# Four chained attention layers: last attention by query halves, reciprocal broadcast on two row groups, sums of x from its update, a new order of steps

## The chip, the cores and the metric

The kernel runs on one core of one Trainium2 chip. TensorE does matrix products out of SBUF into PSUM, ScalarE (ACT) and VectorE (DVE) work on both memories, GpSimd (POOL) on SBUF alone, and the SyncE queue (SP) issues the DMAs. The engines run independently and meet only at semaphores. The metric is the device time of one execution in microseconds (us), lower is better.

## What is computed

x has 2 images of 128 channels by 32x32 positions. Four layers of attention follow each other, each adding its result to x. Positions are 1024 queries and 1024 keys (256 keys in layer 2, which pools 2x2 first).

```python
# layer 0: 4 heads of 4 channels, softmax over the query axis
S = einsum('bhdn,bhdm->bhnm', q, k);  A = softmax(S, axis=-2)
o = einsum('bhdn,bhnm->bhdm', v, A);  x = gamma * (Wo o + bo) + x
# layer 1: one head, 16 channels for q and k, 128 for v
attn = softmax(q k, axis=2);          x = x + gamma * (v attn)
# layer 2: 8 heads of 16; q from group_norm(x), k and v from group_norm(avg_pool2(x))
x = x + wproj @ (softmax(q k * scale) v)
# layer 3: one head of 128 channels on group_norm(x, 32 groups)
x = x + out_w @ (softmax(q k * scale) v) + out_b
```

## The kernel before

**Units.** The work is cut into 17 attention units (L, b, g): layer, image, and a group within the layer (heads in layers 0 and 2; layer 3 of image 0 has its keys split into two units). The last unit is (3, 1, 0). Image 0 runs ahead of image 1, so that at most times two units are in the air.

**Steps of a unit.** The plan is a list of steps, in the kinds of the letters of the string `ORDER` (L89): N are projections q and k, statistics and norm; V is the projection v and one weight fold; A are 8 score tiles whose row maxima VectorE takes out of PSUM (L625 to L636, 1024 elements a row); T turns the maxima into a row (`top`), which a DMA writes next to the operands; B are 8 score tiles, now with the maximum subtracted by the product itself, of which ScalarE takes the exponential into the ring `P` of 13 buffers (L518); P are the products of probabilities and v into `acc` (`PV4` L904 for layers 0 and 2; `PV1` L910 for layers 1 and 3, one per key tile t and half h of the 512 queries), and `out`, the copy of `acc` to SBUF (L529); E is the epilogue. In the epilogue, `den` sums the probabilities on TensorE (L930), VectorE takes the reciprocal and splits it in two parts (L650 to L654), `bcast` spreads it over the channels by 8 products of 128 columns (L939), VectorE multiplies by it and adds to x. In layers 1 and 3 the probabilities are first added up tile by tile into `DS` (L380): on GpSimd for key tiles 1 to 5, on VectorE for 6 and 7.

**What sets the order.** Every engine walks the same list `plan` in its order and takes its own part of each step; nothing is reordered at run time, except that GpSimd only does its sums and SP only its DMAs. Every step that needs PSUM takes the next of three PSUM slots of 1024 columns (`RING`), in plan order; TensorE waits until the step three places before has been read. A new string `ORDER` therefore moves work on TensorE, ScalarE and VectorE at once.

**Places the change touches.** Layer 0's q is masked into two copies (`q0_parity`, L485) on ScalarE after VectorE wrote both halves of it (L598); the first A of a unit waits for the copy (L812). `stats` of layers 2 and 3: ScalarE takes the mean of x (L541, layer 2 only) and its squares (L544) with an accumulating read-out; VectorE pools x (L704 to L710) or, in layer 3, sums x (L699). `norm` (L717 to L744) is a chain of some 15 small VectorE instructions, each waiting for the one before, followed by the scaled copy of x (L550) on ScalarE. x is updated in layer 1 and 3 by L680 (both tensors in SBUF) and in layer 2 by L685 (one tensor in PSUM). The end: the last `out` copies 1024 columns, L674 multiplies, L680 adds, L416 writes 512 KB to memory.

## Time and profile before

| | |
|---|---|
| median of 3 runs | 391.42 us (388.67 to 391.69) |
| the profiled execution | 388.21 us |
| its span, first to last instruction | 386.2 us |
| busy: TensorE, VectorE, ScalarE, GpSimd | 348.5, 255.8, 191.8, 52.4 us |
| mean granted TensorE clock | 0.962 of full speed |

The span is 2.0 us shorter than the execution's own time. Busy time of TensorE is modelled: a matmul's record reaches from its start to its last result, and successive ones overlap, so a row "x8 in 3.43 us" of the chain of waits is the better price of a group than its mean duration. Each fp32 matmul leaves two records. "Idle before" is the idle time of the engine ahead of a row, and the arrow names what ended it.

### The profile page before, as it was taken

To read this page: it belongs to the slowest core of one execution; us is meant where nothing else is said; L and a number is where in the kernel's file an instruction comes from. 1 tells how busy PE (TensorE), PEld (TensorE's weight loads), DVE (VectorE), ACT (ScalarE), POOL (GpSimd) and SP (SyncE) were. 2 spreads that over 40 slices of the span, in tenths; PEclk is the share of its full clock that TensorE was granted. 3 is DMA by queue.
4 is the path that set the end of the run, shared out by engine and by line. 5 is a ranking of instruction groups with operands and counts; after the bars stand their busy time and mean duration, and the time that the engine had idled before them with its cause. 6 is when DMAs were issued, how large, how long until landed. Compare 5 with 4: busy or idle time off the path is not lost.

```text
span 386.2 us, 4574 instructions
## 1 busy us (share of the span) xinstructions
PE 348.5 (90%) x1766; PEld 157.3 (41%) x1766; DVE 255.8 (66%) x315; ACT 191.8 (50%) x234; POOL 52.4 (14%) x36
## 2 busy tenths in 40 slices
PE   8869898999899986999999789969999996999993
PEld 5523322344234432454434335534442453555541
DVE  2799877869878664888773559884981165790424
ACT  4705777685762497545665152256056714224221
POOL 5000000000026300000002142022200022005420
PEclk9955999999999999999999999998999998999998
DMA  8000000000000000000000000000000000000101
GB/s 300 9 0 2 0 3 1 2 0 0 2 0 2 0 0 3 1 3 0 3 0 2 0 0 0 2 0 1 3 2 3 0 0 0 2 0 2 54 0 54
DMA packets 1316, 4.43 MB, mean 11 GB/s; under 512 B 176, under 2 KB 528, under 8 KB 1168
## 3 DMA queue, kind: packets, MB, share of 16 engines
q1 hardware_dynamic: 1296, 4.15, 2.9%
q8 instruction: 14, 0.23, 0.2%
q14 instruction: 6, 0.05, 0.0%
HBM read 2.99 MB, written 1.05 MB: 10 GB/s over the span
## 4 chain that ended last, share of the span: by engine, by line
PE 71%; DVE 18%; ACT 6%; issue 4%; DVEq 0%; ACTq 0%
PE attn_acc L910 13%; PE attn_acc L904 11%; PE products L875 8%; DVE neg_max L632 5%; PE products L879 5%; PE products L825 4%; PE products L864 4%; PE products L793 3%; PE products L869 3%; PE products L797 3%; PE products L838 2%; PE products L939 2%; PE products L805 2%; ACT probs L518 2%; DVE neg_max L635 2%
## 5 line engine op out<-in xcount | busy, mean ns | idle before, releaser
L518 ACT ACTIVATE probs<-products 128x1024 f32<-128x1024 f32 x128 | 126.8, 1022 | 79.2 <-PE products L885 33.7
L632 DVE TENSOR_REDUCE neg_max<-products 128x2 f32<-128x1024 f32 x64 | 75.7, 1219 | 17.6 <-PE products L825 17.6
L910 PE MATMUL attn_acc<-probs,v 128*128 128x512 f32 x128 | 62.7, 607 | 0.0
L904 PE MATMUL attn_acc<-probs,v 128*32 128x512 f32 x384 | 51.1, 612 | 0.4 <-ACT probs L518 0.4
L380 POOL TENSOR_TENSOR prob_sum<-prob_sum,probs 128x1024 f32<-128x1024 f32 x16 | 37.6, 2351 | 77.6 <-ACT probs L518 76.9
L380 POOL TENSOR_TENSOR prob_sum<-probs 128x1024 f32<-128x1024 f32 x4 | 9.4, 2354 | 238.8 <-ACT probs L518 238.8
L635 DVE TENSOR_REDUCE neg_max<-products 128x1 f32<-128x1024 f32 x32 | 37.9, 1220 | 5.7 <-PE products L830 3.7
L629 DVE TENSOR_REDUCE neg_max<-products 128x4 f32<-128x1024 f32 x32 | 37.5, 1217 | 4.5 <-PE products L838 4.4
L910 PEld LDWEIGHTS attn_acc<-probs,v 128*128 128x128 f32 x128 | 22.4, 189 | 21.3 <-issue 18.8
L879 PE MATMUL products<-rows_a,rows_b 128*128 128x512 f32 x64 | 30.5, 599 | 0.6 <-ACT probs L518 0.5
L650 DVE RECIPROCAL recips<-products 128x128 f32<-128x128 f32 x10 | 9.5, 955 | 24.1 <-PE products L930 24.1
L529 ACT ACTIVATE attn_out<-attn_acc 128x512 f32<-128x512 f32 (+1 forms) x16 | 13.0, 814 | 23.3 <-PE attn_acc L910 16.3
L825 PE MATMUL products<-q_even,rounded_a 64*128 64x512 f32 x64 | 17.7, 569 | 3.8 <-DVE neg_max L632 2.6
L864 PE MATMUL products<-rounded_a,q_even 64*128 64x512 f32 x64 | 16.3, 520 | 2.5 <-DVE neg_max L632 1.4
L793 PE MATMUL products<-x_norm,w 128*128 128x512 f32 x16 | 10.3, 729 | 8.9 <-ACT x_norm L550 8.9
L825 PE MATMUL products<-rounded_b,rounded_a 64*128 64x512 f32 x64 | 17.1, 535 | 0.7 <-ACT probs L518 0.5
L380 DVE TENSOR_TENSOR prob_sum<-prob_sum,probs 128x1024 f32<-128x1024 f32 x8 | 9.8, 1221 | 11.2 <-POOL prob_sum L380 6.9
L879 PEld LDWEIGHTS products<-rows_a,rows_b 128*128 128x128 f32 x64 | 11.8, 189 | 12.4 <-issue 10.7
L875 PE MATMUL products<-rows_a,k_rows 64*128 64x512 f32 x64 | 16.3, 612 | 0.5 <-DVE neg_max L629 0.4
L885 PE MATMUL products<-max_rows,max_picker 128*128 128x512 f32 x32 | 16.1, 586 | 0.1
L869 PE MATMUL products<-rows_a,rows_b 64*128 64x512 f32 x64 | 15.9, 606 | 0.0
L864 PE MATMUL products<-rounded_a,rounded_b 64*128 64x512 f32 x64 | 14.1, 458 | 1.9 <-DVE neg_max L632 1.4
(133 smaller groups left out, 410.6 us busy)
## 6 DMA issues: line engine op xcount, KB each, us to landing
w<-w_rest SPq DMA_DIRECT2D x1, 1235.5 KB, 7.5
x<-x SPq DMA_DIRECT2D x2, 512.0 KB, 4.2
y<-x SPq DMA_DIRECT2D x2, 512.0 KB, 2.6
tmp<-row_selector SPq DMA_DIRECT2D x1, 512.0 KB, 8.3
w<-w_first SPq DMA_DIRECT2D x1, 147.0 KB, 2.2
rounded_a<-max_rows SPq DMA_DIRECT2D x8, 4.0 KB
rows_a<-max_rows SPq DMA_DIRECT2D x4, 2.0 KB
rows_a<-max_rows SPq DMA_DIRECT2D x2, 16.0 KB
```

The costliest lines, as they stand in the source:

```text
L380: engine.tensor_tensor(DS[:, :], first_in, P[:, n % NP, :], ALU.add).then_inc(den_acc, 1)
L518: nc.scalar.activation(P[:, n % NP, :], slot(s), ACT.Exp, scale=SCALE[L]).then_inc(read_act, 1)
L629: nc.vector.tensor_reduce(out=m2, in_=slot(s).rearrange("p (a i k) -> p a i k", a=2, i=2), op=ALU.max, axis=AX.X, negate=True).then_inc(re ...
L632: nc.vector.tensor_reduce(out=m[:, 2 * t:2 * t + 2], in_=slot(s).rearrange("p (a n) -> p a n", a=2), op=ALU.max, axis=AX.X, negate=True).t ...
L635: nc.vector.tensor_reduce(out=m[:, t:t + 1], in_=slot(s), op=ALU.max, axis=AX.X, negate=True).then_inc(read_dve, 1)
L825: mm = nc.tensor.matmul(slot(s)[:, halves[a]], RA[b][rows, tile], q0_parity(b, g // 2)[rows, halves[nh]], start=True, stop=True)
L864: mm = nc.tensor.matmul(slot(s)[:, halves[a]], q0_parity(b, g // 2)[rows, 128 * t:128 * (t + 1)], RA[b][rows, halves[g % 2]], start=True, ...
L869: mm = nc.tensor.matmul(slot(s)[:, h], FB[b][rows, 128 * t:128 * (t + 1)], FA[b][rows, h], start=True, stop=True)
L875: mm = nc.tensor.matmul(slot(s)[:, halves[a]], KF2[b][rows, hp, g, 128 * kt:128 * (kt + 1)], (FA, FB)[g][b][rows, halves[half]], start=Tru ...
L879: nc.tensor.matmul(slot(s)[:, h], FB[b][:, 128 * t:128 * (t + 1)], FA[b][:, h], start=True, stop=False)
L904: mm = nc.tensor.matmul(acc[32 * j:32 * j + 32, h], lhs, P[:, b_no[q] % NP, halves[a]], start=t0 == 0 if L == 0 else t0 % 2 == 0, stop=t0 ...
L910: mm = nc.tensor.matmul(acc[:, h], V13[b][:, t0, :], P[:, b_no[q] % NP, h], start=t0 == first, stop=t0 == last)
```

## The change

It has five parts.

1. **Last attention by query halves.** In the last unit all 8 products for queries 0 to 511 are issued first, then those for 512 to 1023. A new step `oh` copies the first half of `acc` in between. Multiply, add and output DMA are done for each half.
2. **Reciprocal broadcast on two 64-row groups.** The 8 products of each `bcast` take 64 rows each and are issued alternately to rows 0 to 63 and 64 to 127.
3. **Sums of x from its update.** The updates of x in layers 1 and 2 also put out the sum of x. ScalarE's pass L541 goes, VectorE's pass L699 becomes a copy of one column; layer 2 gets one small scaling instead.
4. **q masks by halves.** Layer 0's masked copies of q are made by halves, and the first of them waits for the first half of q only.
5. **A new order of steps.**

```diff
 ORDER = (
-    "NNVNNAVAAAAAAAATAAABABABABAABAPTBABPABABAPBABABABA"
...
-    "AAPAPPAAVAPAPTAAAPPABBABBAPABPTBBBPBBBPPBBBBBPEPPP"
-    "EEPBEYENBNPBNNPPAAPPAABAAPAAVPTPPEBBBPBBEPPPPPPBBP"
-    "PPPBPPPPEPEP"
+    "NNVAANANAVAAAAATAAABAABABABAABPTBAABAPBABABAPBABBA"
...
+    "PAAAPAAPVPAAPTAAPAAPBBABBAPABPTBBBPBBPBBBPBBBPEPPP"
+    "EPEYEBENPPNBBNNVAAPAPAAPAABAPPTPPEBBBBBPPBPPPBBPPP"
+    "EEPPPPPPPPEPP"
 )
...
+        if (L, b) == LAST:
+            steps["P"] += [("PV1", L, b, g, t, 0) for t in range(8)] + [("oh", L, b, g)] + [
+                ("PV1", L, b, g, t, 1) for t in range(8)]
...
+                elif kind == "bcast" and (L, b) == LAST:
+                    for i, h in enumerate(halves):
+                        sp.wait_ge(x_upd, x_no[(3, b)] + i)
+                        sp.dma_start(out[b][:, h], X[b][:, h]).then_inc(out_done, 16)
...
-                        wait_read(act, s)
                         for p in range(2):
-                            nc.scalar.activation(q0_parity(b, p)[:, :], RB[b][:, :].bitcast(F32), ACT.Identity,
-                                                 scale=w("group_mask")[:, p:p + 1]).then_inc(q0_masked, 1)
+                            for h in halves:
+                                if p == 0 and h.start == 0:
+                                    act.wait_ge(q0_lo_half, q0_no[s] + 1)
+                                elif p == 0:
+                                    wait_read(act, s)
+                                nc.scalar.activation(q0_parity(b, p)[:, h], RB[b][:, h].bitcast(F32), ACT.Identity,
+                                                     scale=w("group_mask")[:, p:p + 1]).then_inc(q0_masked, 1)
...
+                elif kind == "oh":
+                    u = s[1:]
+                    act.wait_ge(pv_done, half_pv)
...
+                    nc.scalar.activation(O[o_tile[u]][:, halves[0]], acc[:, halves[0]], ACT.Identity).then_inc(half_out, 1)
+                elif kind == "out" and (L, b) == LAST:
+                    u = s[1:]
+                    act.wait_ge(pv_done, pv_done_at[("B", *u, 7)])
+                    nc.scalar.activation(O[o_tile[u]][:, halves[1]], acc[:, halves[1]], ACT.Identity).then_inc(acc_out, 1)
...
-                    if L == 2:
-                        nc.scalar.activation(unused, X[b][:, :], ACT.Identity, scale=1.0 / N,
-                                             accum_out=mv[:, 0, 0:1]).then_inc(act_chain, 1)
-                        act.wait_ge(act_chain, b + 1)
...
+                    elif (L, b) == LAST:
+                        wait_read(dve, ("fold", 3))
+                        if x_upd_before(s):
+                            dve.wait_ge(x_upd, x_upd_before(s))
+                        for i, h in enumerate(halves):
+                            if i == 0:
+                                dve.wait_ge(half_out, 1)
+                            else:
+                                dve.wait_ge(acc_out, out_no[("out", L, b, g)] + 1)
+                            link(nc.vector.tensor_tensor(T[:, h], o[:, h], slot(s)[:, h], ALU.mult))
+                            nc.vector.scalar_tensor_tensor(out=X[b][:, h], in0=T[:, h], scalar=b3eff[:, 0:1],
+                                                           in1=X[b][:, h], op0=ALU.add, op1=ALU.add).then_inc(x_upd, 1)
...
+                            nc.vector.scalar_tensor_tensor(out=X[b][:, :], in0=T[:, :], scalar=gb1[:, 0:1],
+                                                           in1=X[b][:, :], op0=ALU.add, op1=ALU.add,
+                                                           accum_out=xsum[:, b:b + 1]).then_inc(x_upd, 1)
...
-                    nc.vector.tensor_tensor(X[b][:, :], slot(s), X[b][:, :], ALU.add).then_inc(read_dve, 1)
+                    nc.vector.scalar_tensor_tensor(out=X[b][:, :], in0=slot(s), scalar=1.0, in1=X[b][:, :],
+                                                   op0=ALU.mult, op1=ALU.add,
+                                                   accum_out=xsum[:, b:b + 1]).then_inc(read_dve, 1)
...
-                        nc.vector.tensor_reduce(out=mv[:, 0, 0:1], in_=X[b][:, :], op=ALU.add,
-                                                axis=AX.X).then_inc(stats_done, 1)
+                        nc.vector.tensor_copy(mv[:, 0, 0:1], xsum[:, b:b + 1]).then_inc(stats_done, 1)
...
+                    nc.vector.tensor_scalar(mv[:, 0, 0:1], xsum[:, b:b + 1], 1.0 / N, None, ALU.mult)
...
-                            pe.wait_ge(q0_masked, 2 * q0_no[("q", 0, b)] + g // 2 + 1)
+                            pe.wait_ge(q0_masked, 4 * q0_no[("q", 0, b)] + 2 * (g // 2) + 1)
...
+                    if L == 0 and t == 1:
+                        pe.wait_ge(q0_masked, 4 * q0_no[("q", 0, b)] + 2 * (g // 2) + 2)
...
-                    for t in range(NT):
-                        mm = nc.tensor.matmul(slot(s)[:, 128 * t:128 * (t + 1)], selr[:, t, :], RT[:, :],
-                                              start=True, stop=True)
+                    for i in range(NT // 2):
+                        for a in range(2):
+                            t = NT // 2 * a + i
+                            rows = slice(WIDE * a, WIDE * a + WIDE)
+                            mm = nc.tensor.matmul(slot(s)[:, 128 * t:128 * (t + 1)], selr[rows, t, :], RT[rows, :],
+                                                  start=True, stop=True)
```

Written out as steps, these are the stretches of the new order in which the prediction's steps lie (b0 and b1 are the images; steps not named keep their places but for a few swaps of neighbours):

```
start    before  k00 q00 v00 k01 q01 A0 v01 A1 A2 A3 A4
         after   k00 q00 v00 A0 A1 k01 A2 q01 A3 v01 A4
L2 b0    before  q200 k20 B34 out012 v20 PV40130 B35 A0 A1 PV40131
         after   q200 k20 B34 out012 PV40130 PV40131 B35 A0 v20 A1
end L2   before  out201 B0 B1 B2 den201 PV00 ya20 bcast201 PV01 PV10 y20 stats30 B3 PV11 PV20 norm30
 b0      after   out201 B0 den201 B1 B2 B3 bcast201 ya20 PV00 y20 PV01 PV10 PV11 stats30 PV20 norm30
norm21   before  stats21 B3000 B3001 norm21 B3002 PV00 q210
         after   stats21 B3000 B3001 norm21 PV00 PV01 B3002 q210
norm31   before  out211 B3014 bcast211 ya21 y21 stats31 B3015 norm31 PV40 B3016 q31 k31 PV41
         after   out211 den211 ya21 bcast211 B3014 y21 stats31 PV40 PV41 norm31 B3015 B3016 q31 k31 v31
end      before  B0 B1 B2 PV00 B3 B4 bcast301 PV01 .. B7 PV51 PV60 PV61 PV70 den310 PV71 bcast310 out310
         after   B0 .. B4 PV00 PV10 B5 PV20 PV30 PV40 B6 B7 PV50 PV60 PV70 bcast301 den310 oh PV01 .. PV61 bcast310 PV71 out310
```

## Rows read from the trace of the kernel before

**Rows 1.** The page: busy time of each engine, and two lines of slices.
```profile
PE 348.5 (90%) x1766; PEld 157.3 (41%) x1766; DVE 255.8 (66%) x315; ACT 191.8 (50%) x234; POOL 52.4 (14%) x36
PEclk9955999999999999999999999998999998999998
```
**Rows 2.** Windows: us, PE, PEld, DVE, ACT, POOL busy, clock, DMA share, GB/s.
```profile
16.00:48.00 32.00, 25.57 (x110) 10.29 (x111) 28.99 (x30) 14.78 (x16) 0.00 (x0) 0.68 0.00 1
48.00:80.00 32.00, 29.23 (x199) 9.96 (x199) 25.94 (x27) 24.49 (x31) 0.00 (x0) 1.00 0.01 2
```
**Rows 3.** Timeline of the start: start us, us, engine, line, tiles, idle before.
```profile
10.64 1.15 ACT L485 ACTIVATE q_even<-rounded_b,w 128x1024 fp32r<-128x1024 f32 x1 [0.89 <-DVE rounded_b L598]
13.60 1.42 DVE L598 SCALAR_TENSOR_TENSOR rounded_a<-products,w,stage_hi 128x512 fp32r<-128x512 f32 x2 [2.64 <-ACT stage_hi L474]
16.27 1.22 DVE L632 TENSOR_REDUCE neg_max<-products 128x2 f32<-128x1024 f32 x1
```
**Rows 4.** Chain that ended last, pieces in time: start us, us, what.
```profile
123.08 1.06 PE attn_acc L910 x2
203.49 1.04 PE products L939 x8
312.15 0.84 PE products L939 x8
352.50 0.86 PE attn_acc L910 x2
```
**Rows 5.** Timeline: products on two 64-row groups, layer 2.
```profile
280.64 1.04 PE L838 MATMUL products<-k_rounded,rounded_b 64*128 64x256 f32 x12
```
**Rows 6.** Timeline, norm and v of image 0 in layer 2.
```profile
142.78 1.06 ACT L541 ACTIVATE x_norm<-x 128x1024 bf16<-128x1024 f32 x1 [0.21 <-DVE x L680]
144.65 0.22 DVE L710 SCALAR_TENSOR_TENSOR mean_var<-mean_var 128x1 f32<-128x1 f32 x1
145.25 0.36 PE L965 MATMUL products<-mean_var,w 128*128 128x4 f32 x2 [1.51 <-ACT x_norm L544]
154.27 0.71 PE L805 MATMUL products<-w,kv_norm 128*128 128x128 f32 x4 [1.04 <-DVE rows_a L602]
```
**Rows 7.** Timeline, end of layer 2 of image 0, den201 and bcast201.
```profile
209.50 2.35 POOL L380 TENSOR_TENSOR prob_sum<-probs 128x1024 f32<-128x1024 f32 x1 [80.57 <-ACT probs L518]
211.97 2.51 DVE L654 SCALAR_TENSOR_TENSOR recip_rows<-recips_hi,w,recips 128x128 fp32r<-128x128 f32 x1
214.58 1.08 PE L939 MATMUL products<-recip_rows,head_rows_to_channels 128*128 128x128 f32 x8 [2.08 <-issue]
```
**Rows 8.** Timeline, norm30.
```profile
222.58 2.35 POOL L380 TENSOR_TENSOR prob_sum<-prob_sum,probs 128x1024 f32<-128x1024 f32 x1 [8.25 <-ACT probs L518]
222.72 2.22 DVE L732 SCALAR_TENSOR_TENSOR norm_tmp<-norm_tmp,eps 128x1 f32<-128x1 f32 x1
227.98 1.10 PE L793 MATMUL products<-x_norm,w 128*128 128x512 f32 x2 [1.92 <-ACT x_norm L550]
```
**Rows 9.** Timeline, norm31.
```profile
319.93 2.33 DVE L732 SCALAR_TENSOR_TENSOR norm_tmp<-norm_tmp,eps 128x1 f32<-128x1 f32 x1
325.30 1.46 PE L793 MATMUL products<-x_norm,w 128*128 128x512 f32 x2 [2.70 <-ACT x_norm L550]
326.55 1.91 PE L797 MATMUL products<-x_norm,w 128*128 128x512 f32 x2
```
**Rows 10.** Timeline, the end.
```profile
377.67 1.12 PE L910 MATMUL attn_acc<-probs,v 128*128 128x512 f32 x2
378.83 1.02 ACT L529 ACTIVATE attn_out<-attn_acc 128x1024 f32<-128x1024 f32 x1 [4.04 <-PE attn_acc L910]
381.89 1.28 DVE L680 SCALAR_TENSOR_TENSOR x<-tmp,b3eff,x 128x1024 f32<-128x1024 f32 x1
```
**Rows 11.** Groups by line and form: busy us, mean ns.
```profile
L604 DVE TENSOR_SCALAR rows_b<-products,w 128x512 f32<-128x512 f32 x8 | 5.9, 749 | 2.3 <-PE products L793 1.5 <-ACT rounded_b L479 0.6
L529 ACT ACTIVATE attn_out<-attn_acc 128x512 f32<-128x512 f32 x8 | 4.8, 604 | 2.1 <-PE attn_acc L904 2.1
```

More of the change, by code:

```diff
@@ L74 @@
 TILES[(3, 0, 0)], TILES[(3, 0, 1)] = range(0, 4), range(4, 8)
+LAST = (3, 1)
 def groups(L, b):
@@ L138, in build_plan @@
         steps["B"] += [("B", L, b, g, t) for t in TILES[(L, b, g)]]
-        steps["P"] += [("PV4", L, b, g, c) for c in range(4)] if L in (0, 2) else [
-            ("PV1", L, b, g, t, h) for t in TILES[(L, b, g)] for h in range(2)]
+        if (L, b) == LAST:
+            steps["P"] += [("PV1", L, b, g, t, 0) for t in range(8)] + [("oh", L, b, g)] + [
+                ("PV1", L, b, g, t, 1) for t in range(8)]
+        else:
+            steps["P"] += [("PV4", L, b, g, c) for c in range(4)] if L in (0, 2) else [
+                ("PV1", L, b, g, t, h) for t in TILES[(L, b, g)] for h in range(2)]
         steps["P"] += [("out", L, b, g)]
@@ L194, in attention_layers @@
             o_tile[s[1:]] = o_tile[(*s[1:3], s[3] - 1)]
-        elif s[0] == "out":
+        elif s[0] == "oh" or s[0] == "out" and s[1:3] != LAST:
             tile, before = free.pop(0)
@@ L204, in attention_layers @@
     for s in plan:
+        if s[0] == "PV1" and s[1:3] == LAST and s[4:] == (7, 0):
+            n += 1
+            half_pv = n
         if s[0] == "PV4" or s[0] == "PV1" and s[5] == 1:
@@ L270, in attention_layers @@
         eps = sb("eps", [C, 2])
+        xsum = sb("x_sums", [C, B])
         zeros = sb("zeros", [128, NKV])
@@ L293, in attention_layers @@
         acc_out = sem("acc_out")
+        half_out = sem("half_out")
         recip_done = sem("recip_done")
@@ L600, in _ @@
                                 in1=HT[:, split0.index(s) % 2, h].bitcast(F32), op0=ALU.add, op1=ALU.add)
+                            if kind == "q" and h.start == 0:
+                                lo.then_inc(q0_lo_half, 1)
                         elif L == 2:
@@ L911, in _ @@
                                               start=t0 == first, stop=t0 == last)
-                    if kind == "PV4" or s[5] == 1:
+                    if kind == "PV4" or s[5] == 1 or (L, b) == LAST and t0 == 7:
                         mm.then_inc(pv_done, 1)
```

29 lines of the change are left out of this document (18 added, 11 removed).

## Prediction

> **What bounds the kernel now.** I read the page first. TensorE is busy 348.5 of 386.2 us, VectorE 255.8, GpSimd 52.4, and the second line shows the TensorE clock at its lower level, 1.2 GHz, in slices 2 and 3 of 40 (about 19 to 39 us) and dipping near 260 and 325 us [rows 1]. So TensorE sets the time, and what can be won is its idle time, its time at the lower clock, and the ends of the kernel. Next come the windows: from 16 to 48 us VectorE is the fuller engine (28.99 of 32 us against TensorE's 25.57), from 48 to 80 us TensorE is (29.23) [rows 2]. Then the chain of waits, for what a group of products costs back to back [rows 4, 5], and the timeline wherever TensorE idles [rows 3, 6 to 10].
>
> One pattern explains most of those places. A VectorE instruction on one column, normally 0.16 to 0.22 us, takes 2.22 us at 222.72, and it ends at 224.94, as the GpSimd sum that began at 222.58 does (2.35 us) [rows 8]. The same happens to L732 at 319.93 (2.33 us) [rows 9] and to L654, 2.51 us at 211.97, behind a row of GpSimd sums [rows 7]. All of these read SBUF alone. So a GpSimd sum that starts inside a chain of small VectorE instructions costs about 2.1 us, and TensorE pays: it idles 2.08 us before bcast201 [rows 7], 1.92 before norm30's q [rows 8] and 2.70 before norm31's [rows 9]. The step that starts such a sum is a B tile, so the order of steps decides whether they meet.
>
> **q masks by halves, and the start: -1.8 us.** VectorE finishes v00 at about 10.96 us, then idles 2.64 us until 13.60, because ScalarE makes two full masked copies (L485, 1.15 us the first) before it rounds k01; its first maximum starts at 16.27 [rows 3]. In the new order A0 and A1 stand ahead of k01, and the first half mask (about 0.6 us by the 512-wide copy [rows 11]) can start when VectorE has written half of q, some 0.8 us earlier. VectorE can then take two maxima (2 x 1.22 = 2.44 us) in the 2.64 us gap. All else it does up to the eighth maximum stays, and to 48 us it is the fuller engine [rows 2], so the whole is 2.4 us shorter at best. Two extra ScalarE launches are hidden by ScalarE's 14.78 of 32 us. Bounds 0 and -2.6. I take -1.8, since TensorE at 1.2 GHz is near full as well.
>
> **Broadcast on two row groups: -2.0 us.** A bcast is 8 products in 0.84 us between 128-row products and 1.04 us next to 64-row ones [rows 4], so 0.105 us each. Layer 2's products on two row groups, 12 of 256 columns, run in 1.04 us including the 0.27 us of the last one's latency, so 0.07 us each, with twice the columns [rows 5]. Eight of them then take 0.56 us at most; one streaming bound by half the columns gives 0.42. But the rows show a price of changing the row groups: a pair of L910 takes 0.86 us after its like and 1.06 us right after 64-row work [rows 4], 0.2 us a change. For the five or so bcasts next to 64-row work the change goes away, for those inside layer 3 it is added. Gain per bcast 0.1 to 0.5 us, taken as 0.28; of ten, nine count here (the last is in the end's sum), and about seven lie on TensorE's path: -2.0, bounds 0 and -4.
>
> The Trainium skill bears on this: "TensorEngine Tiling (Array Packing)", Key Properties, says that changing the tiling mode drains the engine. The 0.2 us rows agree with it. By that rule alone, bcasts among 128-row products win nothing.
>
> **Sums of x: +0.3 us.** In layer 2 ScalarE's L541 goes (1.06 us plus its read-out), but VectorE's pooling chain beside it ends at 144.65 + 0.22 = 144.87, and the norm product starts at 145.25 [rows 6]. With one small scaling more on VectorE that product starts only 0.1 us sooner. In layer 3 the pass that goes ran beside ScalarE's squares, so nothing is won there either. What is paid is the accumulating read-out on the four updates of x, 0.1 us each from nothing up to the 0.19 us ScalarE's needs by the groups. ScalarE is free 1.2 us earlier, but it only passes on exponentials for which TensorE isn't waiting.
>
> Another price for the update in layer 1, with both tensors in SBUF: the Trainium skill's "Vector Engine (DVE) Microarchitecture Reference", section 7, says such an instruction with two fp32 SBUF inputs and the accumulator runs at half throughput. No row shows one. It is rival 3.
>
> **L2 of image 0, v20 moved back: -0.6 us.** TensorE idles 1.04 us in front of v20, whose slot waits for VectorE [rows 6]. In the new order PV40130 and PV40131 stand there, 1.0 us each and ready. A0 still can't start before 156.4 us (k is then read), so TensorE wins one such product group less the v20 work (0.4 us) that it does later.
>
> **End of layer 2 of image 0: -3.6 us.** den201 now stands behind B0 instead of B2 and ahead of B1, whose exponential starts GpSimd's first sum. TensorE can start it once `out201` is copied, at 207.5 us. Reciprocal 0.96, rounding 0.23, split 0.35 then end near 209.9; B1's exponential would end near 210.2. So L654 runs free of GpSimd, by a margin of about 0.3 us, and B1 to B3 cover the wait: the 2.08 us of idle goes [rows 7]. After that B3 is done before `stats30`, and the next exponential stands behind norm30 in ScalarE's list, so no GpSimd sum falls into norm30's chain: 2.1 us less there, and the 1.92 us of idle goes [rows 8]. Together 4.0 us; 3.6 for crumbs. Bounds -0.3 (both holds come back) and -4.2.
>
> **norm21: -0.5 us.** One more PV stands between norm21 and q210, where TensorE idles 2.7 us, but the idle 0.46 ahead of norm21 is untouched and GpSimd's first sum still falls into the chain, earlier by about the time that ScalarE saves. Bounds 0 and -1.7 (the clock's dip at 260 us spared).
>
> **norm31: -2.8 us.** B3014 moves ahead of y21, and B3015, whose exponential started the sum that held L732, moves behind norm31 in every list. The chain ends 2.1 us sooner, and PV40, PV41 fill the wait for the statistics. Now q31 starts at 325.30 after 2.70 us of idle, and its second product pair takes 1.91 us where the same work takes 0.86 at 2.4 GHz: the granted clock there is at its lower level after the idle time [rows 9]. I put q31 at 323.8 (-1.5), one PV more done by then (-0.86), and about half of the 1.9 us that the lower clock costs the four products as spared. That is 3.3; 2.8 taken, bounds -1 and -4.5.
>
> **The end: -2.4 us.** Now from the end of the last PV (377.67 + 1.12 = 378.79) follow copy, bcast, multiply and add, until 381.89 + 1.28 = 383.17: 4.38 us [rows 10]. Then 3.0 us of DMA end the span. After: half copy 0.60 [rows 11], half multiply 0.7, half add 0.75 (as the 512-wide 0.749 of L604 [rows 11]), handoffs 0.15: 2.2 us, so -2.2. The last bcast now comes ahead of the last PV on TensorE (+0.5), and den310 no longer makes TensorE wait (0.76 us), as bcast301 is put ahead of it and covers the last sum: -0.7. The final DMA carries half; I leave its 3.0 us, since a latency may be all of it (else -0.6). The first half's DMA and image 0's, which is later now than at 362 us but still behind a full PV half of about 6 us, are hidden.
>
> **Sum.** -1.8 - 2.0 + 0.3 - 0.6 - 3.6 - 0.5 - 2.8 - 2.4 = -13.4, from the profiled 388.21: 374.8. The runs' median is 3.2 us above that execution, their lowest 0.5. A median of the new kernel may lie as high above its fastest, so I add 1.2: **376.0 us**. Its own range is 371 to 380.
>
> **Rivals.** Of the bounds above, no one alone changes the sign.
> 1. **Forecast**, chance 0.50.
> 2. **GpSimd's holds come back elsewhere**, 0.20. The margin at den201 is 0.3 us, and earlier exponentials make earlier sums. Two holds of 2.1 us with the idle time behind them give back 5: 381. For: the same holds at 211, 222 and 320 us. Against: the lists keep B behind the two norms.
> 3. **The accumulator halves the layer 1 update**, 0.10: L680 at 1.28 us [rows 10] becomes 2.56, twice on the path: 376.0 + 2.6 = 378.6. The Trainium skill's page named above would give this.
> 4. **Dependences take most of it**, 0.12. VectorE has 28.99 of 32 us in 16 to 48, so that start and norms move but their followers wait for VectorE. Start, v20, norm21 and half of norm31 and of the bcasts gone: 376 + 1.8 + 0.6 + 0.5 + 1.4 + 1.0 = 381.3; with rival 2 on top up to 386. This includes that splitting into row groups does nothing.
> 5. **The clock stays low**, 0.08, the case on the other side. It is at 1.2 GHz from 19 to 39 us while VectorE bounds. If the new mix of A and B keeps it there into 48 to 80, where TensorE is busy 29.23 of 32 us, each microsecond of its work costs nearly one more. From 14 us longer at the lower level it decides; 20 us give about 394.
>
> The range holds forecast and rivals 2 to 4: 369 to 386. About 1% is what can be told from no change here, so below 387.5 is faster: 0.85; within 1% 0.08 (rivals 4 and 5 mild); slower 0.07.
>
> **What would show it.** The first L632 near 11 to 12 us instead of 16.27. Bcasts of 0.5 to 0.6 us, and L910 pairs of 1.06 behind them in layer 3. L654 of bcast201 at 0.35 us and no idle before it; L732 at 0.16 us in norm30 and norm31, still one held op in norm21. No L541. L680 of layer 1 near 1.3 us, or 2.6 by rival 3. At the end 2.2 us from the last PV to the last add. I am wrong if the slices of the clock show the lower level past slice 3, or if TensorE's idle time before its q products stays.

## The result

| | before | after |
|---|---|---|
| median of 4 runs | 390.05 us (388.36 to 391.69) | 375.77 us (373.23 to 375.94) |
| the profiled execution | 388.21 us | 375.87 us |
| its span | 386.2 us | 373.8 us |
| mean granted TensorE clock in it | 0.962 | 0.965 |

The ratio is 0.961, with an interval of 0.956 to 0.967: 3.9% faster. The forecast of 376.0 us (range 369 to 386) holds. But it is a sum of eight terms, and what follows asks which of them were right. Two failed in this profile: the start, whose gain came out only in executions where the clock stayed up, and v20. The price of the sums of x was never separated, and the end was near in size with wrong parts.

To see where the time went I compare the starts of the same steps in the two profiled executions. The differences between columns are worked out from the timelines.

| step | before | after | ahead by |
|---|---|---|---|
| first maximum (VectorE) | 16.27 | 11.79 | 4.5 |
| fold behind the eighth maximum | 25.63 | 26.06 | -0.4 |
| norm product, layer 2 of image 0 | 145.25 | 145.20 | 0.0 |
| bcast200 | 203.42 | 203.65 | -0.2 |
| bcast201 | 214.58 | 210.56 | 4.0 |
| q30 | 227.98 | 223.24 | 4.7 |
| norm21 | 254.08 | 249.10 | 5.0 |
| q210 | 260.94 | 255.81 | 5.1 |
| norm31 | 319.09 | 312.78 | 6.3 |
| q31 | 325.30 | 317.44 | 7.9 |
| first B of the last unit | 345.68 | 335.63 | 10.0 |
| end of the last PV | 378.79 | 369.24 | 9.5 |
| end of the last add | 383.17 | 371.38 | 11.8 |
| end of the span | 386.2 | 373.8 | 12.4 |

So between these two executions nothing at all is won in the first 203 us, and everything in the last 170. This is the page of the kernel after, its engines and its clock, to set beside [rows 1]:

```profile
PE 344.5 (92%) x1766; PEld 153.3 (41%) x1766; DVE 244.8 (65%) x323; ACT 191.3 (51%) x235; POOL 52.4 (14%) x36
PEclk9875899999999999999999999998999999999998
```

TensorE is still the engine that bounds. Of the two dips of the clock behind norms, near 260 and 325 us before, one is left, the single 8 in the 28th slice, 252 to 262 us.

**The start** (timeline of after, columns as in [rows 3]):

```profile
11.79 2.36 DVE L663 TENSOR_REDUCE neg_max<-products 128x2 f32<-128x1024 f32 x2 [0.18 <-PE products L876]
13.91 1.91 PE L846 MATMUL products<-x,w 128*128 128x512 f32 x2
15.03 0.75 DVE L627 SCALAR_TENSOR_TENSOR rounded_a<-products,w,stage_hi 128x512 fp32r<-128x512 f32 x1 [0.88 <-ACT stage_hi L490]
16.73 0.75 DVE L627 SCALAR_TENSOR_TENSOR rounded_a<-products,w,stage_hi 128x512 fp32r<-128x512 f32 x1 [0.95 <-ACT stage_hi L490]
```

Two maxima do stand in the gap of [rows 3], as forecast. Then VectorE waits twice, 0.88 and 0.95 us, for k01's halves. The granted clock fell here: k01's second pair of records (L846) takes 1.91 us, where it takes 1.02 in the kernel before.

**The end of layer 2 of image 0, and the norm behind it** (timeline of after), to set beside [rows 7, 8]:

```profile
209.66 0.35 DVE L685 SCALAR_TENSOR_TENSOR recip_rows<-recips_hi,w,recips 128x128 fp32r<-128x128 f32 x1
210.56 2.37 POOL L392 TENSOR_TENSOR prob_sum<-probs 128x1024 f32<-128x1024 f32 x1 [82.02 <-ACT probs L538]
210.56 0.96 PE L993 MATMUL products<-recip_rows,head_rows_to_channels 64*128 64x128 f32 x8
...
220.04 0.16 DVE L781 SCALAR_TENSOR_TENSOR norm_tmp<-norm_tmp,eps 128x1 f32<-128x1 f32 x1
...
223.24 1.10 PE L842 MATMUL products<-x_norm,w 128*128 128x512 f32 x2
```

The split (L685 now) takes 0.35 us for 2.51 and is through 0.55 us before GpSimd's first sum starts; the one-column instruction takes 0.16 us for 2.22; TensorE idles neither before the broadcast nor before norm30's q.

**norm31 and norm21** (timeline of after), to set beside [rows 9]:

```profile
250.40 2.34 POOL L392 TENSOR_TENSOR prob_sum<-probs 128x1024 f32<-128x1024 f32 x1 [20.77 <-ACT probs L538]
250.47 2.41 DVE L776 SCALAR_TENSOR_TENSOR norm_tmp<-norm_tmp 128x1 f32<-128x1 f32 x2
255.81 2.05 PE L842 MATMUL products<-x_norm,w 128*128 128x512 f32 x2 [2.43 <-ACT x_norm L579]
...
313.62 0.16 DVE L781 SCALAR_TENSOR_TENSOR norm_tmp<-norm_tmp,eps 128x1 f32<-128x1 f32 x1
317.44 1.02 PE L842 MATMUL products<-x_norm,w 128*128 128x512 f32 x2
```

In norm21 one instruction is still held, as forecast, and TensorE idles 2.43 us behind it; its next pair of records takes 2.05 us. norm31 is free of it, and its pair takes 1.02 us.

**Sums of x** (timeline of after):

```profile
141.41 1.28 DVE L724 SCALAR_TENSOR_TENSOR x<-tmp,gamma_bv,x 128x1024 f32<-128x1024 f32 x1
142.62 0.08 DVE L724 DVE_READ_ACCUMULATOR x<-tmp,gamma_bv,x 128x1 f32 x1
```

The update with both tensors in SBUF takes 1.28 us as it did without the accumulator, and the read-out 0.08 us.

**The end** (chain that ended last, pieces in time: start us, us, what), to set beside [rows 10]:

```profile
360.23 0.59 PE products L993 x8
360.82 0.57 PE products L981 x16
361.39 6.21 PE attn_acc L961 x14
367.60 0.59 PE products L993 x8
368.19 1.07 PE attn_acc L961 x2
...
369.28 0.61 ACT attn_out L551
...
369.91 0.70 DVE tmp L710
...
370.63 0.75 DVE x L711
```

The pieces left out are of 0.02 us. From the last PV to the last add it is 2.1 us instead of 4.4. The DMA behind is 2.4 us (371.38 to 373.8) instead of 3.0, and its landing is on the page:

```profile
y<-x SPq DMA_DIRECT2D x1, 512.0 KB, 2.6
y<-x SPq DMA_DIRECT2D x2, 256.0 KB, 2.0
```

**One thing is needed to read the numbers below.** Executions of one and the same kernel differ by whole dips of the TensorE clock, that is stretches in which the granted clock falls toward its lower level, and such differences come to 2.5 us and more. Of the kernel before, six of the 13 executions measured along with experiment 1 have a mean granted clock of 0.961 or 0.962 and take 387.6 to 388.6 us; seven have 0.950 to 0.957 and take 391.4 to 393.1. Of the kernel after, one has 0.971 and takes 373.2 us, three have 0.965 and take 375.7 to 375.9. So medians carry luck of some 3 us, and I compare, beside the medians, executions of like mean clock or the fastest of each kernel, and steps of one profile against each other. The mean doesn't say where a dip lies, though: the profiles of experiments 1 and 6 have one at 152 to 164 us, where neither before nor after has one, and in experiment 4 the executions at a mean of 0.953 are faster than those at 0.958. A difference read at like clock is therefore good to about 1 us, and step distances are the better evidence. The lowest times of the two kernels in this comparison are 388.4 and 373.2 us, 15.1 apart (14.3 against 387.6, the lowest of before anywhere); the two profiled executions are 12.3 apart.

### The profile page after: what moved, and what is told of

Its sections match the earlier page's. It is cut to its first block, busy times and chain, and to the rows that moved or that the text cites. A ratio compares the mean times of both kernels' runs of the same rounds, so it can differ in the third digit from the quotient of the medians.

```text
span 373.8 us, 4592 instructions
## 1 busy us (share of the span) xinstructions
PE 344.5 (92%) x1766; PEld 153.3 (41%) x1766; DVE 244.8 (65%) x323; ACT 191.3 (51%) x235; POOL 52.4 (14%) x36
## 4 chain that ended last, share of the span: by engine, by line
PE 75%; DVE 14%; ACT 6%; issue 4%; ACTq 0%; DVEq 0%
PE attn_acc L961 13%; PE attn_acc L955 11%; PE products L926 7%; PE products L930 7%; PE products L915 5%; PE products L876 5%; PE products L842 4%; PE products L846 4%; PE products L920 4%; DVE neg_max L660 3%; DVE neg_max L663 3%; DVE neg_max L666 3%; ACT probs L538 3%; PE products L854 2%; PE products L1010 2%
## 5 line engine op out<-in xcount | busy, mean ns | idle before, releaser
L538 ACT ACTIVATE probs<-products 128x1024 f32<-128x1024 f32 x128 | 126.7, 1024 | 79.4 <-PE products L936 32.2
L562 ACT ACTIVATE attn_out<-attn_acc 128x512 f32<-128x512 f32 (+1 forms) x15 | 12.0, 800 | 17.1 <-PE attn_acc L961 11.6
L915 PE MATMUL products<-rounded_a,rounded_b 64*128 64x512 f32 x64 | 14.3, 464 | 1.6 <-ACT probs L538 1.0
L926 PE MATMUL products<-rows_b,k_rows 64*128 64x512 f32 x64 | 15.4, 605 | 0.0
```

What stands on the lines that cost most here:

```text
L538: nc.scalar.activation(P[:, n % NP, :], slot(s), ACT.Exp, scale=SCALE[L]).then_inc(read_act, 1)
L915: mm = nc.tensor.matmul(slot(s)[:, halves[a]], q0_parity(b, g // 2)[rows, 128 * t:128 * (t + 1)], RA[b][rows, halves[g % 2]], start=True, ...
L926: mm = nc.tensor.matmul(slot(s)[:, halves[a]], KF2[b][rows, hp, g, 128 * kt:128 * (kt + 1)], (FA, FB)[g][b][rows, halves[half]], start=Tru ...
```

## The experiments

### 1. The order against the rest

Two kernels split the change. The first is the kernel before with the new string up to the last unit:

```diff
 ORDER = (
-    "NNVNNAVAAAAAAAATAAABABABABAABAPTBABPABABAPBABABABA"
...
+    "NNVAANANAVAAAAATAAABAABABABAABPTBAABAPBABABAPBABBA"
...
```

> The kernel before, with the new order of steps up to the last unit and nothing else of the change. By the prediction the order carries the start (in part), the end of layer 2 of image 0, v20, norm21 and norm31: 388.2 - 7 to - 9, about 380. The traces of the two kernels say that nothing is won up to bcast200 at 203 us and 9 us from there to the first B of the last unit: bcast201 near 210.6, norm30's q near 223.5 to 224, the last unit's first B near 337 to 338 instead of 345.7, time 379 to 381. The rival, that the row groups and the sums of x carry the gain, expects over 385.

Measured: 381.78 us (381.44 to 383.18), 0.980 of before (0.974 to 0.986). The second has the row groups, the sums and the half masks, but the old order and end (here in its one line that differs beside the string):

```diff
-LAST = (3, 1)
+LAST = (9, 9)
```

> The new row groups of the broadcast, the sums of x from the update and the q masks by halves, with the old order and the old end. By the prediction -2.0 for the row groups and +0.3 for the sums: 386.5. By the traces of the two kernels the broadcasts are 0.2 to 0.3 us shorter each, the updates longer by 0.1, and little of it lies on the path: 386 to 388. If the parts carried the gain: under 383.

Measured: 385.39 us, in two pairs: 383.8 and 383.9 at a clock of 0.962, 386.9 twice at 0.957; 0.989 of before (0.982 to 0.995). At the clock of 0.962 the kernel before takes 388.2 (its middle), so these parts win 4.3 us, not the 1.7 that I had put down and not the 0 to 2 of the expectation. The row groups have 2.1 of it (experiment 6). The other 2 us are not assigned by any run: masks and sums were not run alone. The profile shows two candidates. The masks by halves bring the fold behind the eighth maximum 0.24 us nearer to v00 (16.61 us behind v00's first product, 16.85 before). And from norm31's product to the end of the span it is 64.4 us instead of 67.1: the held instruction costs 0.4 us less (norm31's product to q31 in 5.77 us for 6.21), and the clock stays at 1.00 behind it, where it dipped in the profile of before. Whether the new sums spare that dip or this execution merely drew none is open.

The order alone wins 6.6 at equal clock (381.5 against 388.1), less than the 7 to 9 of the expectation and than the 9.3 of the terms that it carries. The steps say where that goes: from bcast200 to the first B of the last unit its profile has 131.95 us, as after (131.98) and 10.3 less than before (142.26), but it reaches bcast200 only at 207.55, with a low clock at 12 to 16 and at 152 to 160 us. With the end's 1.8 (experiment 7) the three differences make 12.7, near the 12.3 of the two profiled executions; as each is good to about 1 us, that they add up so well is in part luck.

### 2. The end of layer 2 of image 0, alone and undone

The new order of these steps put into the kernel before:

```diff
-    "BBABAAPANAVNTPBABABABABAPAPBBAPABEPTBBEPPPBBBEPYEP"
-    "PENBPPNBBPPNNBBAAPAPAPAPAPPPPAPEAPVETNBBNBPNNNBAAP"
+    "BBABAAPANAVNTPBABABABABAPAPBBAPABEPTBBEPPPBEBBBEYP"
+    "EPPPNPNBBPPNNBBAAPAPAPAPAPPPPAPEAPVETNBBNBPNNNBAAP"
```

These are the steps of the stretch "end L2 b0".

> The kernel before, with 12 steps in the new order: from behind B0 to norm30 at the end of layer 2 of image 0 (den201 ahead of B1, B3 ahead of the broadcast). Theory (GpSimd's sums held L654 and L732): L654 at 0.35 us, L732 at 0.16 us, TensorE's 2.08 and 1.92 us of idle time gone, norm30's q near 224 instead of 228, and the same 3.5 to 4.5 us at the end: about 384.3. Rival (the gain is given back behind, since VectorE or GpSimd bounds the next stretch): norm30's q at 224, but under 2 us at the end.

Measured: 386.45 us (382.24 to 387.04), 0.989 of before (0.981 to 0.997). In its profile no L654 above 0.35 us and no held L732 in norm30. From bcast200 to norm21 it takes 253.59 - 207.26 = 46.33 us, where before takes 254.08 - 203.42 = 50.66: 4.3 us. From bcast200 to the last add it is 173.75 for 179.75; the 1.7 more are a dip behind norm21 that this execution doesn't have and before has. At 0.957, the clock of two of its executions, it takes 386.9, before 391.4: 4.5.

The same steps undone in the changed kernel:

```diff
-    "BAPABBAAPANBTPAAVBABABBAPAPBBAPABEPTBBEPPPBEBBBEYP"
-    "EPPPNPNBBPPNPNBB...
+    "BAPABBAAPANBTPAAVBABABBAPAPBBAPABEPTBBEPPPBBBEPYEP"
+    "PENBPPNBBPPNPNBB...
```

> The changed kernel with the 12 steps at the end of layer 2 of image 0 in the old order (den201 behind B2, B3 behind stats30). By the prediction 3.6 us more, by the two traces 4 to 4.7: 377 beside 373.2 where the clock's dip near 256 us stays away, 379.5 to 380 beside 375.8 where it comes; L685 held to 2.5 us and L781 to 2.2 us again. Rival (the gain is one of idle time that another stretch would have had): under 2 us.

Measured: 381.98 us (378.29 to 382.37). Best against best 378.29 - 373.23 = 5.1 us, by the medians 6.2; the steps are worth more than the 3.6 forecast. The holds are back (timeline of this kernel):

```profile
209.01 2.35 POOL L392 TENSOR_TENSOR prob_sum<-probs 128x1024 f32<-128x1024 f32 x1 [81.04 <-ACT probs L538]
210.30 1.14 DVE L684 CAST recips_hi<-recips 128x128 fp32r<-128x128 f32 x1
211.47 2.51 DVE L685 SCALAR_TENSOR_TENSOR recip_rows<-recips_hi,w,recips 128x128 fp32r<-128x128 f32 x1
214.09 0.66 PE L993 MATMUL products<-recip_rows,head_rows_to_channels 64*128 64x128 f32 x8 [2.08 <-issue]
221.82 2.34 POOL L392 TENSOR_TENSOR prob_sum<-prob_sum,probs 128x1024 f32<-128x1024 f32 x1 [7.98 <-ACT probs L538]
221.96 2.23 DVE L781 SCALAR_TENSOR_TENSOR norm_tmp<-norm_tmp,eps 128x1 f32<-128x1 f32 x1
```

The same two idle times of TensorE, 2.08 us here and 1.92 before q30, return with them. Put in or taken out, the steps are worth 4.3 to 5.1 us, so the gain belongs to them and isn't given back behind them.

### 3. Are the holds GpSimd's doing?

```diff
-POOL_SUM = 6
+POOL_SUM = 1
```

All sums of probabilities go to VectorE, in the kernel before:

> The kernel before with all sums of probabilities on VectorE (POOL_SUM 1 for 6), GpSimd idle after its memsets. Theory (GpSimd's sums hold VectorE instructions that read SBUF alone): L653 and L654 at 0.23 and 0.35 us, L732 and L740 at 0.16, and q30, q210, q31 each about 2 us sooner. VectorE does 20 sums of 1.22 us more, 24 us, some of it in the way where it is full: between 381 and 390. Rival (something else holds them, a semaphore of the chain or the PSUM): they stay at 2.2 us.

Measured: 386.33 us (385.33 to 386.51), 0.989 of before (0.983 to 0.995), at a clock of 0.952 to 0.953. No instruction of the chains is held (timeline of this kernel):

```profile
214.26 0.35 DVE L654 SCALAR_TENSOR_TENSOR recip_rows<-recips_hi,w,recips 128x128 fp32r<-128x128 f32 x1
224.04 0.16 DVE L732 SCALAR_TENSOR_TENSOR norm_tmp<-norm_tmp,eps 128x1 f32<-128x1 f32 x1
227.24 1.10 PE L793 MATMUL products<-x_norm,w 128*128 128x512 f32 x2 [0.28 <-ACT x_norm L550]
```

The stretches behind the norms shrink by what the holds cost: from norm21's product to q210 4.72 us for 6.86, from norm31's to q31 4.04 for 6.21. With 24 us more of sums on VectorE (its busy time rises by 10.6 only, 266.4 for 255.8) this kernel is 1% faster than the one before. In the changed kernel the same edit (POOL_SUM = 1 for 6) has little left to win:

> The same in the changed kernel, where one instruction is still held (2.41 us in norm21). Theory: that one falls to 0.35, q210 comes 2 us sooner and the clock's dip behind it goes, for 2 to 4 us less, against 24 us more of VectorE work in layers 1 and 3, where the new order has put no room for it: 371 to 378. In the last unit the sums have time (VectorE idles 18.7 us ahead of the sixth).

Measured: 381.37 us (380.46 to 381.69), 5.6 us slower than the changed kernel and above what I expected. norm21's hold is gone, but norm21 itself comes later: from bcast201 it is 42.6 us away (253.16 - 210.57) instead of 38.5. The sums of layer 1's image 1 now stand among the maxima of layer 3's image 0 on VectorE, and TensorE idles 2.53 us before `den` (L981, at 241.28) for the last of them. So the holds are GpSimd's, shown in both kernels, and the cure depends on the order: before, take the sums away from GpSimd; after, move their start.

Not every instruction is held. In experiment 4's second kernel a GpSimd sum runs from 311.68 to 314.06; two one-column instructions of the form TENSOR_SCALAR inside it take 0.15 and 0.14 us (L783, L785, at 311.88 and 311.95), and the SCALAR_TENSOR_TENSOR behind them is held for 1.95. The prediction's words "all of these read SBUF alone" are true of the held ones, but it is not enough to be held.

The Trainium skill has the rule: "GPSIMD Engine Reference", sections 1 and 8, says that GpSimd shares its SBUF interfaces with VectorE and contends with instructions that have two SBUF inputs or run in a two-port mode. The trace agrees for two inputs (L732 at 2.22 us). The cast L653 has one input and takes 1.14 us beside a sum, 0.23 elsewhere; whether it runs in a two-port mode no row shows. A hold costs here what is left of a sum of 2.35 us.

### 4. norm31 alone and undone

The new order from norm31 on to the last unit, put into the kernel before:

```diff
-    "EEPBEYENBNPBNNPPAAPPAABAAPAAVPTPPEBBBPBBEPPPPPPBBP"
+    "EPEYEBENPPNBBNNVAAPAPAAPAABAPPTPPEBBBPBBEPPPPPPBBP"
```

> The kernel before, with the steps between the last broadcast of layer 2 of image 1 and the last A of the last unit in the new order. By the prediction -2.8, by the two traces -3.3 to -3.7 (no held L732, no lower clock over the q products, v31 in the wait for the first A): about 384.7. Rival (most of it came from the shorter broadcasts and the lower clock spared by chance): under 1.5 us.

Measured in ten executions: four take 384.7 to 385.2 us at a clock of 0.965, four 388.5 to 389.1 at 0.953, two 389.9 at 0.958; 0.992 of before (0.987 to 0.997). Its fast four against the fast six of before that is 3.2 us less (384.9 against 388.1). From norm31's product to the last PV's end its profile has 55.95 us, before 59.70: 3.75, and it has no dip behind norm31.

And the reverse in the changed kernel:

```diff
-    "EPEYEBENPPNBBNNVAAPAPAAPAABAPPTPPEBBBBBPPBPPPBBPPP"
+    "EEPBEYENBNPBNNPPAAPPAABAAPAAVPTPPEBBBBBPPBPPPBBPPP"
```

> The changed kernel with the steps from the last broadcast of layer 2 of image 1 to v31 in the old order. By the prediction 2.8 us more, by the two traces 3.3 to 3.7: 376.5 to 377 with no dip at 256 us, 379 with one; L781 held in norm31, and a dip of the clock behind it. Rival (the order only moved idle time): under 1.5 us.

Measured: 376.99 us (375.17 to 377.59), by the medians 1.2 us more than after, below the 1.5 that the rival would leave. But medians mix dips. Its best is 1.9 us above the best of after, and its profiled execution, with a dip of the clock behind norm31 as in [rows 9] and none behind norm21, is 4.0 above. In that profile the held instruction and what follows it are these:

```profile
312.13 1.95 DVE L776 SCALAR_TENSOR_TENSOR norm_tmp<-norm_tmp 128x1 f32<-128x1 f32 x1
316.60 2.05 PE L842 MATMUL products<-x_norm,w 128*128 128x512 f32 x2 [2.26 <-ACT x_norm L579]
318.44 1.80 PE L846 MATMUL products<-x_norm,w 128*128 128x512 f32 x2
```

So the steps are worth the hold, about 1.9 us, and about 2 more in executions where the clock would have dipped.

### 5. The start

The old first ten steps in the changed kernel:

```diff
-    "NNVAANANAVAAAAATAAAB...
+    "NNVNNAVAAAAAAAATAAAB...
```

> The changed kernel with the first ten steps in the old order; masks of q by halves stay. By the prediction the start was worth 1.8 us: 377.7. By the trace of the changed kernel, whose eighth maximum is no sooner than before (26.06 us against 25.63) since k01 and q01 run at 1.2 GHz there, it is worth nothing: 375.9, with the eighth maximum at 26.0 to 26.5.

Measured: 373.42 us (372.96 to 376.22), of which three at a clock of 0.971, where after has one (373.23). Equal at equal mean clock. I count the start from v00's first product, since the kernels' first products come at 5.06 to 5.62 us. The fold behind the eighth maximum is 16.62 us behind it with the old start, 16.63 in the profile of after, 16.85 in the kernel before. In that profile the start's new order is worth nothing.

Why? In the changed kernel the clock fell to 0.65 in 12 to 16 us, under k01's products. So I kept TensorE busy there with products whose results are unused:

```diff
-    "NNVAANANAVAAAAATAAAB...
+    "NNVAWAWNWAWNAVAAAAATAAAB...
```

> The changed kernel with four idle products (128x256, fp32, 0.43 us each at 2.4 GHz, results unused) after A0, A1, k01 and A2 of the first unit, nothing else. Theory: the start won nothing because TensorE's clock fell at about 12.6 us, when it had only v00's 16-column products and waits; kept busy it stays at 2.4 GHz until q01 is done, the eighth maximum comes at 24 to 25 us instead of 26.06 and the whole is 1 to 2 us shorter. Rival (the start is bound by ScalarE's rounding and masks): the eighth maximum stays at 26, or moves later by the added products.

Measured: 375.83 us (372.84 to 376.29), no change. The clock did stay at its upper level (windows of this kernel: us, TensorE busy, clock, DMA share, GB/s):

```profile
12.00:16.00 4.00, 4.00 (x14) 1.00 0.00 0
16.00:20.00 4.00, 4.00 (x21) 1.00 0.00 0
```

and the fold still came at 26.00 us. VectorE's waits in that kernel: 1.11 us in ScalarE's wait for k01's product, 1.07 in VectorE's for the rounding, then 1.57 and 0.47 us for q01. A0 and A1 wait for the masks on TensorE, and k01, which stood right behind v00 before (10.2 to 10.5 us), is queued behind them until 12.6.

This looks like the end of the theory of the clock, but the test changes two things: the idle products stand ahead of k01 and q01. k01 starts 3.87 us behind v00 here, and 3.16 in after; q01 7.08, and 7.04 in after with its slow clock. The theory has a cleaner test in two kernels run for other reasons, which have the same first unit as after: the one with the old end (experiment 7) and the one without GpSimd's sums (experiment 3). In both the clock stayed up by itself. The windows, after first, then the old end and no GpSimd sums:

```profile
12.00:16.00 4.00, 3.84 (x8) 0.65 0.00 0
12.00:16.00 4.00, 3.59 (x12) 1.00 0.00 0
12.00:16.00 4.00, 3.60 (x11) 1.00 0.00 0
```

And the rows of the one with the old end (timeline; v00's first product is at 9.73, k01's at 12.90, q01's at 15.24):

```profile
13.86 1.02 PE L846 MATMUL products<-x,w 128*128 128x512 f32 x2
14.94 1.61 DVE L627 SCALAR_TENSOR_TENSOR rounded_a<-products,w,stage_hi 128x512 fp32r<-128x512 f32 x2 [0.49 <-ACT stage_hi L490]
24.89 0.17 DVE L674 TENSOR_TENSOR max_folds<-neg_max 128x8 f32<-128x8 f32 x1
```

The fold is 15.16 us behind v00's first product here and 15.15 in the other, 1.7 us nearer than in the kernel before and 1.5 nearer than with the old start. In this kernel the gain lasts up to norm20's product, 133.73 us behind v00's first product, where the old start has 135.42. In the four other profiles with this start and the masks by halves (after, and the kernels of experiments 2, 4 and 6 that undo one part) the clock falls to 0.57 to 0.65 in 12 to 16 us, and the fold is 16.63 to 16.85 behind. So the new start is worth what was forecast when the clock stays up under k01, and nothing when it falls. Of the 2.4 us that the two maxima fill, the chain product, rounding, subtraction of k01 and q01 takes back 0.9 with the clock up and all with it down. What makes the clock fall there in some executions is open.

### 6. The broadcast over all rows again

```diff
-                    for i in range(NT // 2):
-                        for a in range(2):
-                            t = NT // 2 * a + i
-                            rows = slice(WIDE * a, WIDE * a + WIDE)
-                            mm = nc.tensor.matmul(slot(s)[:, 128 * t:128 * (t + 1)], selr[rows, t, :], RT[rows, :],
-                                                  start=True, stop=True)
+                    for t in range(NT):
+                        mm = nc.tensor.matmul(slot(s)[:, 128 * t:128 * (t + 1)], selr[:, t, :], RT[:, :],
+                                              start=True, stop=True)
```

> The changed kernel with the broadcast's 8 products over all 128 rows again. By the prediction 2.0 us more: 377.9. Per broadcast 0.84 us in layer 3 and 1.04 beside 64-row products, against 0.59 and 0.45 now; a pair of PV products right behind one in layer 3 at 0.86 instead of 1.06. Rival (the change of row groups eats the gain): the same time within 0.5 us.

Measured: 377.98 us, all four within 0.4 at a clock of 0.964 or 0.965, where after takes 375.7 to 375.9: 2.1 us, the 2.0 forecast. The two profiles have their dip in different places (156 to 164 us here, 252 to 260 in after), so this is good to about 1 us; the pieces below show the same gain by themselves. The pieces of the chains, this kernel first:

```profile
206.11 1.04 PE products L990 x8
369.84 0.84 PE products L990 x8
```

and after, at the same two places:

```profile
204.22 0.40 PE products L993 x8
367.60 0.59 PE products L993 x8
```

Beside work of narrow row groups a broadcast costs 0.40 us instead of 1.04, inside layer 3 0.59 instead of 0.84, and there a pair of PV behind it 1.07 us instead of 0.93 (370.68 in this kernel's chain). The change of row groups is paid in layer 3, as forecast, but doesn't eat the gain.

### 7. The old end

```diff
-LAST = (3, 1)
+LAST = (9, 9)
...
-    "EPEYEBENPPNBBNNVAAPAPAAPAABAPPTPPEBBBBBPPBPPPBBPPP"
-    "EEPPPPPPPPEPP"
+    "EPEYEBENPPNBBNNVAAPAPAAPAABAPPTPPEBBBPBBEPPPPPPBBP"
+    "PPPBPPPPEPEP"
```

> The changed kernel with the last unit as before: no query halves, old order from its first B on. By the prediction the end is worth 2.4 us, by the two traces 2.3 (10.05 us ahead at the first B of the last unit, 12.35 at the end): 378 us beside 375.9, with 4.4 us from the last PV to the last add instead of 2.2. Rival (the end's gain is a gain of the whole, by less work behind it): under 1 us.

Measured: 374.95 us (374.36 to 377.82), by the median less than after, which says nothing, since after has its dip in three of four executions. At a clock of 0.972 it takes 374.4 and 374.6, after at 0.971 takes 373.2: 1.1 to 1.4 us. But its profiled execution is one of the two in which the start won 1.5 us. The better measure is the stretch from norm31 to the end of the span: 62.8 us here, 61.1 in the kernel with the old start and 61.0 in after: 1.8. It is below the 2.4 forecast, and not near nothing. Its chain at the point in question:

```profile
363.64 0.65 PE L981 MATMUL products<-prob_sum,w 128*32 128x128 f32 x16
364.21 1.13 PE L961 MATMUL attn_acc<-probs,v 128*128 128x512 f32 x2
```

The PV ahead of L981 runs from 360.11 in eight records of 0.43 us, to 363.55. TensorE does not wait there for more than 0.1 us.

## Why the prediction was right or wrong

**The whole** was right, and by more luck than it looks: -13.4 was forecast against the profiled execution, -12.3 measured between the profiled ones, and the 1.2 added for the median made up the rest. Measured on medians the change is -14.3, since the median of before lay high. The terms that failed in these profiles (1.8, 0.6 and 0.6 of the end) are balanced by those that were too small (3.6 for 4.3 to 5.1, and 2.8 for 3.7 between the two profiles).

**The start, -1.8: right in size where the clock stays up (1.7 in two profiles), nothing in the others.** The step that failed is "All else it does up to the eighth maximum stays". It counted VectorE's work and not the chain that feeds it. Two maxima ahead of k01 put two TensorE steps that wait for masks ahead of k01's products, and these then lie on VectorE's path; whether they run at the upper or the lower clock decides the rest. In the profile of after the gap of 2.64 us came back in four parts (0.88 and 0.95 us in the rows above, the rest at q01). The prediction named what is queued behind a moved step for other places and not here, and it put the slow clock behind 19 us, not in front of it. That 1.7 comes so near to 1.8 is luck: the 0.6 held back was meant for TensorE being near full.

**Broadcast, -2.0: right** in size (2.1), with single gains outside my range of 0.1 to 0.5 on one side: 0.64 us where no change of row groups is left, 0.1 to 0.25 in layer 3. The Trainium skill's rule of draining ("TensorEngine Tiling (Array Packing)", Key Properties), by which layer 3 would win nothing, describes a price that is there but smaller than the gain.

**Sums of x, +0.3: not shown, and perhaps of the wrong sign.** What was priced, the read-out, is 0.08 us, not 0.1 to 0.19, and the norm product of image 0 comes no later. But no run has the sums alone, and experiment 2 leaves some 2 us of gain for sums and masks that the prediction put at nothing. Rival 3 is refuted: 1.28 us with the accumulator as without, where half throughput would have made it 2.56. That the Trainium skill's page "Vector Engine (DVE) Microarchitecture Reference", section 7, states half throughput for this form does not hold here.

**v20, -0.6: wrong.** The 1.04 us of idle time did go, and the two products stand there, but TensorE then idled 0.94 us ahead of A0, which waited for k until 156.4 as I had said. The work that came forward wasn't missed later: from the norm product to bcast200 it is 58.45 us, before 58.17. The step that failed is "TensorE wins one such product group": A0 waits for k whatever stands before it, so idle time filled ahead of v20 opened again ahead of A0. This edit was not run alone, so its worth is read from two profiles and not shown by an experiment.

**End of layer 2, -3.6: right in mechanism, too small.** Both holds and both idle times went, shown by putting the steps in (4.3), taking them out (5.1), and by taking GpSimd's sums away. The margin that I gave as 0.3 us was 0.55. The 0.4 that I held back "for crumbs" was earned, and more.

**norm21, -0.5: too large,** 0.15 by the two profiles (6.86 us from norm21 to q210, now 6.71). The hold stayed, as I had said. The dip behind it is there in the profiles of after and of the kernel with idle products, and not in those with the old start, the old end, the old broadcast and the two undone orders, which have the same hold (2.3 us).

**norm31, -2.8: right,** between 1.9 without and 4.0 with a dip of the clock spared; the prediction had put half of the dip's cost into the sum.

**The end, -2.4: the size nearly, the parts not.** Copy, multiply and add by halves give 2.24 (2.2 forecast) and the broadcast in front of the last PV costs 0.6 (0.5). But the 0.7 for den310's wait did not exist: the 0.76 us that I took is idle time of the weight load, which precedes those products, and in the trace TensorE waits 0.1 us there (377.0 to 377.10, by the records). The half-size DMA, which I left at 3.0 us, is 0.6 shorter. One error covered most of the other: experiment 7 gives 1.8 for the whole. Against the kernel before, the stretch from the last unit's first B to the end of the span is 2.4 us shorter (38.2 for 40.5), but the shorter broadcasts are in that as well.

**Rivals.** Rival 2 (holds come back elsewhere) did not happen; one hold stays where it was. Rival 4 happened for the first 203 us only, and only in executions like the profiled one of after. Rival 5: the clock was low to about 40 us, as before, and not beyond.

## What to carry to other kernels

A small VectorE instruction that takes exactly as long as the rest of a GpSimd instruction is being held by it; find which step starts the GpSimd work and put it behind the chain, which here was worth over 6 us of 14. When a step is moved forward into a gap of one engine, follow the step that it displaces through all engines: the gap was filled here and reopened behind it, in part with the clock up and wholly with it down. A test that adds work to hold the clock up also moves what stands behind that work; look first for an execution in which the clock stayed up by itself. Take idle time from the row of the engine itself (PE, not its weight load). Where executions differ by more than what is measured, compare step distances in stretches of like granted clock; an equal mean clock alone is not enough.

## What the runs showed of the hardware

- The same kernel draws dips of the TensorE clock by execution. In experiment 4 the same program ran at mean clocks of 0.965, 0.958 and 0.953, for 384.8, 389.9 and 388.8 us. In the changed kernel the dip lies behind norm21, where TensorE had worked 1.57 of 4 us; in the profile with the old start it had worked 1.56 of 4 at that place and the clock stayed up. The rows, the profile of after first and the one with the old start second (windows: us, TensorE busy, clock, DMA share, GB/s):

```profile
252.00:256.00 4.00, 1.57 (x6) 0.94 0.01 2
256.00:260.00 4.00, 4.00 (x8) 0.63 0.00 0
```

```profile
252.00:256.00 4.00, 1.56 (x5) 1.00 0.00 2
256.00:260.00 4.00, 4.00 (x13) 1.00 0.00 0
```

- What decides between the two is open; the rows show like activity ahead of both.
- The same holds at the start: with the same first unit the clock fell to 0.57 to 0.65 in 12 to 16 us in four profiles and stayed at 1.00 in two, and the first eight maxima took 1.5 to 1.7 us less in these.
- A running GpSimd sum (2.35 us) holds one-column SCALAR_TENSOR_TENSOR instructions of VectorE to its end (1.95 to 2.33 us for 0.16 to 0.22) and lets one-column TENSOR_SCALAR ones pass (0.15 us).
- A DVE update of 1024 fp32 columns with both inputs in SBUF gives its sum for 0.08 us more.
- Eight products of 128 columns on alternating 64-row groups take 0.40 us beside other narrow groups and 0.59 us beside 128-row products.
